# Attention in two-part float32: scores computed once with queries on the partitions, probabilities transposed on TensorE

## The chip, the cores and the metric

The kernel runs on one core of a Trainium2 chip. The metric is the device time of one execution in microseconds, as the median of several runs. The trace shown here is one profiled execution. PE is TensorE (the matrix engine), DVE is VectorE, ACT is ScalarE, POOL is GpSimd, SP is the engine that issues DMAs.

## The reference

The input is x of shape (2, 1024, 256). It is normalised over its last axis (xn). Two branches read xn, and both are added to x:

```python
# attention: 16 heads of 192 (128 without rotation, 64 with rotary embedding)
q_latent, kv_latent = xn @ wq_down, xn @ wkv_down        # 192 and 64 wide
q = concat([q_latent @ wq_nope, rope(q_latent @ wq_rope)])
k = concat([kv_latent @ wk_nope, rope(kv_latent @ wk_rope)])
v = kv_latent @ wv_up
scores = q k^T / sqrt(192), masked causally
out = softmax(scores) @ v                                # per head
attention = out.reshape(b, t, 16 * 192) @ wo
# feed-forward: 32 experts of 96, top 8 by a softmax over gate logits
ffn = sum over experts of routing * (silu(xn @ gate) * (xn @ up)) @ down
```

## The kernel before

The work has three blocks, one after the other: `prepare` (line 69: normalisation, transposes, the latents), `attend` (line 399: attention, and the routing weights beside it) and `mix` (line 1103: the experts). Only `attend` and small parts of `prepare` are touched.

**Numbers in two parts.** Where float32 precision is wanted from a fast product, a tensor is kept as a high part (type float32r, written by a copy on ACT) and a low part (what is left, a subtraction on DVE or POOL). A product is then three matmuls: high with high, high with low, low with high. A matmul whose operands are plain float32 takes two records in the trace and twice the time for a column.

**Folded weights.** For a head, the key's part without rotation is folded into the query's projection, so that scores without rotation are a product of a 64-wide folded query with the 64-wide key-value latent. With the 64 rotated rows this makes 128 rows, one full contraction. Values are the latent itself (`kvn`, 64 wide); the value weights are folded with `wo`.

**Stages.** A stage is one pair of heads (eight pairs) and one batch element (two): sixteen stages `s`. Pair 0 and the last pair are written out, pairs 1 to 6 are a loop. In a stage PE goes through 12 steps (`step_of`, line 347), each for one block of 128 keys and a chunk of up to 512 queries, keys on the partitions: for either head a score product of three matmuls (lines 599 to 601), a bfloat16 product that subtracts the row maximum from the whole column (line 598: ones times a diagonal matrix of maxima), and on the diagonal a mask product (line 597). ACT takes the exponential into a ring of three buffers (line 734). The values product (line 613) of the step before follows, both heads at once in two 64-column halves of the array. DVE and POOL add the probabilities of the two heads into `first` (lines 908 and 1060); a product with ones gives the row sums (line 634), DVE takes the reciprocal of 128x512 (line 913) and multiplies (line 917).

**Maxima.** They are wanted before the step's scores. So each stage also computes, for the next one, a high-with-high score product with queries on the partitions, in 24 pieces of up to 512 keys (line 566, mask in line 569), whose maximum DVE takes (line 897); ACT turns them into the diagonal matrices (line 770). `PIECE_AT` (line 378) says by hand after which step each piece stands. The first stage's 24 pieces run before the loop.

**Side work.** Between the steps stand products for the next stage, by the table `SIDE` (line 382): QR0, QR1 (rotated query of chunk 0 and 1), KR0, KR1 (rotated key), QL0, QL1 (folded query), L0 and Lp (row sums of chunk 0, and of chunk 1 of the stage before), Y0, Y1, Yp0, Yp1 (output products), B and WA (weight folds, in every other stage). They alternate between two PSUM banks `ps_x`; each waits until the one two before it is consumed. A rotated product is consumed by DVE (lines 850 and 851), then POOL (lines 1029 and 1031), then split by ACT (lines 757 and 758) and POOL (line 1047). A folded query is split by ACT (lines 750 and 751) and DVE (lines 858 and 860). WA is consumed by DVE in lines 867 to 872, B in lines 877 and 879, output products in line 923.

Every engine works through its own queue in the order in which its function of the block is written.

Of the kernel before, what the change touches and what calls it, by code (L numbers as in the profile page):

```python
# [26 lines left out]
AXX = mybir.AxisListType.X  # L27
# [7 lines left out]
P = 128  # L35
# [33 lines left out]
def prepare(nc, d, keep):  # L69

    ctx = ExitStack()
    with ctx:
# [22 lines left out]
        def _(sp):  # L95
# [7 lines left out]
            for name, to in (("cos", keep["cosv"]), ("sin", keep["sinv"]), ("ones", keep["ones"]), ("mask", keep["raw_mask"])):  # L103
                sp.dma_start(to[:, :], d[name]).then_inc(ahead_loaded, 16)
# [6 lines left out]
            sp.wait_ge(ahead_loaded, 16 * 6)  # L111

        @block.vector
        def _(dve):
# [27 lines left out]
            def low_parts(g):  # L142
# [4 lines left out]
                for count, lo, ps, hi in (  # L147
# [6 lines left out]
                    nc.vector.tensor_tensor(lo, ps, hi.bitcast(F32), ALU.subtract).then_inc(lo_done, 1)  # L154

            def split_first_weights():

                dve.wait_ge(ahead_loaded, 16 * 6)
# [22 lines left out]
        def _(act):  # L181
# [14 lines left out]
            for g in range(NCH):  # L196
# [8 lines left out]
                nc.scalar.activation(keep["kv"][:, s], ps_l[2][:, :], ACT.Copy).then_inc(hi_copied, 1)  # L205
                nc.scalar.activation(keep["khi"][b][0][64:P, cs], ps_l[2][64:P, :], ACT.Copy).then_inc(hi_copied, 1)
                nc.scalar.activation(keep["khi"][b][1][0:64, cs], ps_l[2][0:64, :], ACT.Copy).then_inc(hi_copied, 1)
# [4 lines left out]
                if g == 1:  # L212

                    act.wait_ge(ident_loaded, 16)
                    act.wait_ge(ahead_loaded, 16 * 6)
                    for to, of in (("ident16", "ident"), ("ones16", "ones"), ("mask16", "raw_mask")):
                        nc.scalar.activation(keep[to][:, :], keep[of][:, :], ACT.Copy).then_inc(consts16_done, 1)
# [6 lines left out]
        def _(pe):  # L224
# [13 lines left out]
            for g in range(NCH):  # L238
# [18 lines left out]
                if g == 1:  # L257
# [3 lines left out]
                    pe.wait_ge(ahead_loaded, 16 * 6)  # L261
# [26 lines left out]
STEPS = 12  # L288
PROLOGUE = ["QR0", "KR0", "QL0", "QR1", "KR1", "QL1"]
STAGE = ["QR0", "KR0", "QR1", "KR1", "Lp", "QL0", "QL1", "L0", "Yp0", "Yp1", "B", "WA", "Y0", "Y1"]  # L290


def misc_order(first=False, last=False):
# [3 lines left out]
    for b in range(B):  # L297
        for name in STAGE:
# [4 lines left out]
            got.append((b, name))  # L303
    return got
# [7 lines left out]
def misc(i, b, name):  # L312

    if b is None:
        n = PROLOGUE.index(name)
        return n, n % 2
    if isinstance(i, int) and i == 0:
        n = len(PROLOGUE) + FIRST.index((b, name))
        return n, n % 2
    if isinstance(i, int) and i == PAIRS - 1:  # L320
        n = BEFORE_LAST + LAST.index((b, name))
        return n, n % 2
    pos = LATER.index((b, name))
    if isinstance(i, int):
        n = AFTER_FIRST + len(LATER) * (i - 1) + pos
        return n, n % 2
    return i * len(LATER) + (AFTER_FIRST - len(LATER) + pos), (AFTER_FIRST + pos) % 2


def misc_predecessor(i, b, name):  # L330

    if b is None:
        at = PROLOGUE.index(name) - 2
        return (0, None, PROLOGUE[at]) if at >= 0 else None
    if isinstance(i, int) and i == 0:
        at = FIRST.index((b, name)) - 2
# [1094 lines left out]
```

## Time and profile before

| | us |
|---|---|
| median of 3 runs (1276.21 to 1277.69) | 1276.71 |
| the profiled execution, its own time | 1277.71 |
| its span, first to last instruction | 1275.9 |
| mean granted clock of TensorE | 0.985 |

The span is what the rows show; 1.8 us lie around it. A matmul's recorded duration includes its way through the array and overlaps the next one: what it costs is read from the distance between starts. Names in the rows leave buffer numbers out, and the tile `keys` is a first buffer that holds `khi` and `klo` of batch 0, `xtf` holds the shuffled half of a rope product, and `t` is `t1`.

### The profile page before, as it was taken

The numbers are of one execution on the slowest core, as the hardware profiler recorded it, in microseconds if no ns is written. First come the engines' busy times: TensorE is split into PE (matmuls) and PEld (weight loads), VectorE is DVE, ScalarE is ACT, GpSimd is POOL, SyncE is SP. The second block draws the span as 40 slices with busy tenths as digits, with TensorE's granted clock in tenths as the row PEclk, the third lists the DMA queues.
The fourth block names the chain that finished last, engine by engine and source line by source line (L and its number), as shares of the span: only waits on it lengthen the run. The fifth ranks groups of instructions, "written<-read, shape, count | busy, mean of one in ns | idle before, by whom it ended". The sixth has DMA issues, their size and how long they took to land. (4 is left out here: it accounts for less than half of the span.)

```text
span 1275.9 us, 20266 instructions
## 1 busy us (share of the span) xinstructions
PE 1216.7 (95%) x5952; PEld 809.1 (63%) x5952; DVE 898.6 (70%) x1410; ACT 589.5 (46%) x1192; POOL 682.0 (53%) x546
## 2 busy tenths in 40 slices
PE   5899899999999999999999999979999999999997
PEld 3555465555565555555655555547888887888886
DVE  6679879879889888888888798664544444544444
ACT  3454536545546445456355365443434343333332
POOL 1176667677677667767776676552233333233332
PEclk9988999999999999999999999998999999999999
DMA  5001001001000000000000001006533334433332
GB/s 202 34 1 33 1 1 33 1 1 32 0 0 17 15 0 15 16 0 2 30 0 0 15 0 58 1 26 180 163 115 107 110 115 114 127 109 115 115 115 90
DMA packets 26442, 67.33 MB, mean 53 GB/s; under 512 B 3044, under 2 KB 9700, under 8 KB 26408
## 3 DMA queue, kind: packets, MB, share of 16 engines
q1 hardware_dynamic: 26264, 66.84, 17.4%
q8 instruction: 17, 0.28, 0.1%
q14 instruction: 17, 0.14, 0.0%
q10 hardware_dynamic: 144, 0.07, 0.0%
HBM read 62.42 MB, written 4.47 MB: 52 GB/s over the span
## 5 line engine op out<-in xcount | busy, mean ns | idle before, releaser
L734 ACT ACTIVATE ring<-ps_s 128x512 f32<-128x512 f32 (+3 forms) x320 | 146.5, 468 | 302.3 <-PE ps_s L601 301.2
L1333 POOL TENSOR_TENSOR hl<-hf,hh 128x512 fp32r<-128x512 f32 x96 | 123.5, 1286 | 288.2 <-ACT hh L1270 288.2
L897 DVE TENSOR_REDUCE nm<-ps_m 128x1 f32<-128x512 f32 (+3 forms) x370 | 197.8, 550 | 47.0 <-PE ps_m L569 42.1
L1060 POOL TENSOR_TENSOR first<-first,ring 128x512 f32<-128x512 f32 (+3 forms) x160 | 159.5, 997 | 83.8 <-ACT ring L734 51.2
L1029 POOL TENSOR_TENSOR xtf<-xtf,sinv 128x512 f32<-128x512 f32 x62 | 85.3, 1375 | 119.3 <-DVE xtf L851 119.3
L1302 DVE TENSOR_TENSOR gs<-gs,routing 128x512 f32<-128x512 f32 x64 | 44.3, 692 | 137.8 <-ACT gs L1266 137.8
L908 DVE TENSOR_TENSOR first<-first,ring 128x512 f32<-128x512 f32 (+3 forms) x160 | 133.1, 832 | 9.7 <-ACT ring L734 4.9
L613 PE MATMUL ps_o<-ring,kvn 128*64 128x512 f32 (+3 forms) x640 | 132.6, 493 | 0.0
L598 PE MATMUL ps_s<-shift,ones 128*128 128x512 bf16 (+3 forms) x384 | 126.7, 330 | 0.2 <-ACT first L734 0.2
L1270 ACT ACTIVATE hh<-hf 128x512 fp32r<-128x512 f32 x96 | 60.7, 633 | 122.0 <-DVE hf L1307 122.0
L1266 ACT ACTIVATE gs<-ps_g 128x512 f32<-128x512 f32 x96 | 57.4, 598 | 121.4 <-PE ps_g L1225 121.4
L913 DVE RECIPROCAL rec<-ps_x 128x512 f32<-128x512 f32 x32 | 107.3, 3354 | 5.1 <-PE ps_x L634 3.1
L1047 POOL TENSOR_TENSOR qlo<-t,qhi 64x512 fp32r<-64x512 f32 x64 | 94.9, 1483 | 8.6 <-POOL first L1060 2.6
L599 PE MATMUL ps_s<-qhi,keys 128*128 128x512 f32 (+1 forms) x192 | 93.2, 485 | 0.0
L599 PE MATMUL ps_s<-qhi,khi 128*128 128x512 f32 (+1 forms) x192 | 92.1, 480 | 0.0
L1031 POOL TENSOR_TENSOR t<-t,xtf 128x512 f32<-128x512 f32 x62 | 84.5, 1362 | 4.9
L850 DVE TENSOR_TENSOR t<-ps_x,cosv 128x512 f32<-128x512 f32 x64 | 44.2, 691 | 57.1 <-PE ps_x L550 57.1
L566 PE MATMUL ps_m<-khi,qhi 128*128 128x512 f32 (+1 forms) x192 | 73.5, 393 | 7.6 <-DVE nm L897 7.6
L1064 POOL TENSOR_TENSOR olo<-on,ohi 128x512 fp32r<-128x512 f32 x31 | 42.4, 1368 | 70.0 <-ACT ohi L782 70.0
L1307 DVE TENSOR_TENSOR hf<-gs,ps_u 128x512 f32<-128x512 f32 x96 | 66.1, 688 | 10.6 <-PE ps_u L1225 1.3
L566 PE MATMUL ps_m<-keys,qhi 128*128 128x512 f32 (+3 forms) x178 | 68.3, 397 | 5.2 <-DVE nm L897 4.8
L566 PEld LDWEIGHTS ps_m<-khi,qhi 128*128 128x128 f32 x192 | 36.6, 191 | 55.4 <-DVE nm L897 45.7
(241 smaller groups left out, 3104.3 us busy)
## 6 DMA issues: line engine op xcount, KB each, us to landing
routing<-wT_scratch SPq DMA_DIRECT2D x34, 256.0 KB, 3.7
raw_a<-in_e SPq DMA_DIRECT2D x17, 384.0 KB, 3.0
cosv<-in_e SPq DMA_DIRECT2D x17, 384.0 KB, 3.0
sinv<-wT_scratch SPq DMA_DIRECT2D x17, 384.0 KB, 3.6
raw<-in_e SPq DMA_DIRECT2D x17, 384.0 KB, 3.0
routing<-wT_scratch SPq DMA_DIRECT2D x16, 384.0 KB, 3.3
raw_a<-in_a SPq DMA_DIRECT2D x8, 512.0 KB, 3.4
raw_b<-in_b SPq DMA_DIRECT2D x8, 480.0 KB, 4.0
```

The lines of the kernel that those rows point to most:

```text
L566: mm = nc.tensor.matmul(out[:, 0:keys], qhi[b][e][:, t * P:(t + 1) * P], khi[b][e][:, k0:k0 + keys], start=True, stop=not diagonal)
L598: nc.tensor.matmul(out[:, off:], ones16[:, :], shift[:, c, e, off:], start=not diagonal, stop=False, skip_group_check=True)
L599: nc.tensor.matmul(out[:, off:], khi[b][e][:, kk], qhi[b][e][:, q], start=False, stop=False, skip_group_check=True)
L613: nc.tensor.matmul(ps_o[64 * e:64 * e + 64, off:], kvn[:, b * 8 + j, :], probs(k, e), start=j == 0, stop=last).then_inc(pv_done, 1)
L734: nc.scalar.activation(probs(k, e), ps_s[(2 * k + e) % 3][:, off:], ACT.Exp, scale=SCALE).then_inc(exp_done, 1)
L897: nc.vector.tensor_reduce(out=to, in_=bank[:, 0:keys], axis=AXX, op=ALU.max, negate=True).then_inc(piece_max, 1)
L908: nc.vector.tensor_tensor(first[:, c, 0, off:], first[:, c, 0, off:], probs(k, 0), ALU.add).then_inc(sum_dve, 1)
L913: nc.vector.reciprocal(rec[:, :], ps_x[x][:, :]).then_inc(rec_done, 1)
L1029: nc.gpsimd.tensor_tensor(sh[:, g, :], sh[:, g, :], sinv[:, c * CH:(c + 1) * CH], ALU.mult).then_inc(rope_sin, 1)
L1047: nc.gpsimd.tensor_tensor(lo[to_b][e][rows, cs], t1[rows, g, :], hi[to_b][e][rows, cs].bitcast(F32), ALU.subtract).then_inc(rope_lo, 1)
L1060: nc.gpsimd.tensor_tensor(first[:, c, 1, off:], first[:, c, 1, off:], probs(k, 1), ALU.add).then_inc(sum_pool, 1)
L1333: nc.gpsimd.tensor_tensor(hl[:, c, :], hf[:, c, :], hh[:, c, :].bitcast(F32), ALU.subtract).then_inc(h_lo, 1)
```

## The change

Scores are computed once, with queries on the partitions. A stage now goes through eight tiles `t` of 128 queries; for each head all keys up to the diagonal stand side by side in two PSUM banks (two halves from tile 4 on), three matmuls to a half. DVE takes one negated maximum over the row, ACT the exponential with it as bias and with its sum accumulated in the same instruction. In the next tile PE transposes the probabilities in blocks of 128, ACT copies those of one bank (`ps_t[0]`) and DVE those of the other (`ps_t[1]`) into `pt`, and one values product for each key block and head follows. The reciprocals of the sums (128 by 16 numbers) are widened on ACT, transposed on PE (L0 and Lp now) and copied on ACT. The pieces, the shift products, the sums on DVE and POOL, `first`, `ring` and `shift` are gone. Side work has one bank `ps_x`, each waiting for the one just before it; the six of the prologue have banks of their own. The scale of the scores is put on the key-value latent in `prepare`; the constant `ones` is no longer loaded. The transposes of the routing weights take the places of the last stage's first four projections. `mix` is unchanged.

The diff, cut to its core:

```diff
-                nc.scalar.activation(keep["kv"][:, s], ps_l[2][:, :], ACT.Copy).then_inc(hi_copied, 1)
+                nc.scalar.activation(keep["kv"][:, s], ps_l[2][:, :], ACT.Copy, scale=SCALE).then_inc(hi_copied, 1)
...
+            def scores(i, b, t, e, half):
+                s = i * 2 + b
+                u = s * U + 2 * t + e
+                halves = halves_of(t)
+                if half == 0:
+                    ge(pe, exp_done, u - 1)
...
+                if diagonal:
+                    nc.tensor.matmul(out[:, width - P:width], mask16[:, :], ident16[:, :], start=True, stop=False, skip_group_check=True)
+                nc.tensor.matmul(out[:, 0:width], qhi[b][e][:, q], khi[b][e][:, kk], start=not diagonal, stop=False, skip_group_check=True)
+                nc.tensor.matmul(out[:, 0:width], qhi[b][e][:, q], klo[b][e][:, kk], start=False, stop=False, skip_group_check=True)
+                mm = nc.tensor.matmul(out[:, 0:width], qlo[b][e][:, q], khi[b][e][:, kk], start=False, stop=True, skip_group_check=True)
+            def turn(s, t, e, g):
+                x = g if t >= TPC else e
+                before = s * TURNS_PER_S + turns_before(t) + (e if t >= TPC else 0)
+                pe.wait_ge(exp_done, s * U + 2 * t + e + 1)
+                ge(pe, copied[x], before)
+                for at, j in enumerate(groups_of(t)[g]):
+                    mm = nc.tensor.transpose(ps_t[x][:, at * P:(at + 1) * P], prob[t % 2][e][:, j * P:(j + 1) * P], ident[:, :])
+                mm.then_inc(turned[x], 1)
+            def values(s, b, t):
+                for x in range(2):
+                    pe.wait_ge(copied[x], s * TURNS_PER_S + turns_before(t + 1))
+                if t % TPC == 0:
+                    ge(pe, on_done, s * 2 + t // TPC)
+                at = slice(t % TPC * P, (t % TPC + 1) * P)
+                for j in range(t + 1):
+                    for e in range(2):
+                        mm = nc.tensor.matmul(ps_o[64 * e:64 * e + 64, at], kvn[:, b * 8 + j, :], pt[t % 2][:, e, j, :], start=j == 0, stop=j == t)
...
+                    for t in range(TILES):
+                        sp, bp, tp = before_tile(i, b, t)
+                        has = earlier or t > 0
+                        if t == 0:
+                            scores(i, b, t, 0, 0)
+                            if has:
+                                turn(sp, tp, 0, 0)
+                                turn(sp, tp, 0, 1)
+                            scores(i, b, t, 1, 0)
+                            also("Lp")
+                            if has:
+                                turn(sp, tp, 1, 0)
+                                turn(sp, tp, 1, 1)
+                                values(sp, bp, tp)
+                            also("QR0")
+                        elif t < TPC:
+                            scores(i, b, t, 0, 0)
+                            turn(sp, tp, 0, 0)
+                            turn(sp, tp, 1, 0)
+                            scores(i, b, t, 1, 0)
+                            values(sp, bp, tp)
+                            also(("KR0", "QL0", "QR1")[t - 1])
+                        elif t == TPC:
+                            scores(i, b, t, 0, 0)
+                            turn(sp, tp, 0, 0)
+                            scores(i, b, t, 0, 1)
+                            also("L0")
+                            turn(sp, tp, 1, 0)
+                            scores(i, b, t, 1, 0)
+                            scores(i, b, t, 1, 1)
+                            values(sp, bp, tp)
+                            also("Yp0")
+                        else:
+                            scores(i, b, t, 0, 0)
+                            turn(sp, tp, 0, 0)
+                            scores(i, b, t, 0, 1)
+                            turn(sp, tp, 0, 1)
+                            also(("KR1", "Yp1", "WA")[t - TPC - 1])
+                            scores(i, b, t, 1, 0)
+                            turn(sp, tp, 1, 0)
+                            turn(sp, tp, 1, 1)
+                            scores(i, b, t, 1, 1)
+                            if t == TILES - 1:
+                                also("Y0")
+                            values(sp, bp, tp)
+                            also(("QL1", "B", "Y1")[t - TPC - 1])
...
+                nc.scalar.activation(prob[t % 2][e][:, 0:len(halves) * width].rearrange("p (h k) -> p h k", k=width),
+                                     ps_s[e][:, 0:len(halves), 0:width], ACT.Exp, bias=nm[:, e:e + 1],
+                                     accum_out=lsum[:, t // TPC, t % TPC, e:e + 1]).then_inc(exp_done, 1)
...
+                nc.vector.tensor_reduce(out=nm[:, e:e + 1], in_=ps_s[e][:, 0:len(halves), 0:halves[0][1]], axis=AXXY, op=ALU.max,
+                                        negate=True).then_inc(max_done, 1)
...
+                nc.vector.tensor_copy(pt[t % 2][:, e, blocks[0]:blocks[-1] + 1, :].rearrange("p j q -> p (j q)"),
+                                      ps_t[1][:, 0:len(blocks) * P]).then_inc(copied[1], 1)
...
+                nc.vector.tensor_tensor(on[:, :], ps_o[:, :], rec[:, :], ALU.mult).then_inc(on_done, 1)
```

TPC is 4, TILES is 8, and in names like QR0 the digit is the chunk. `sp, bp, tp` is the tile before. From tile 5 on, and in tile 0, the blocks of the tile before are turned in two groups for each head, the first into `ps_t[0]` and the second into `ps_t[1]`; for the tiles 0 to 3 there is one group for each head, head 0's into `ps_t[0]` and head 1's into `ps_t[1]`. `values` waits for all of them.

The order that the new functions give the other engines in a tile:

- ACT: `widen` (tiles 0 and 4); the copy from `ps_t[0]` of head 0; the exponential of head 0; `take_reciprocals` (0 and 4); the copy from `ps_t[0]` of head 1 (0 and 5 to 7); the exponential of head 1; then `out_hi` (1 and 6), `latent_hi` (2 and 5), `rope_hi`, which is four split copies (4 and 7).
- DVE: `invert` (0 and 4); `latent_low(1)` (6); the maximum of head 0; one copy from `ps_t[1]`; the rope products of KR1 (5), the addition of Yp1 (6), the split of WA (7, batch 0); the second copy from `ps_t[1]` (5 to 7); the maximum of head 1; the second copy (0); `normalise` (0 and 4); the rope products of QR0, KR0, QR1 (0, 1, 3) or `latent_low(0)` (2); the additions of Yp0 (4), Y0 and Y1 (7), the split of B (6, batch 0).
- POOL: `rope_sum` 0, `out_low` of the stage before, `rope_sum` 1 and 2, `rope_low` 0 and 1, `rope_sum` 3, `out_low`, `rope_low` 2 and 3.

## Rows read from the trace of the kernel before

**Rows 1.** The page, part 1: busy us, share of the span, instructions.

```profile
PE 1216.7 (95%) x5952; PEld 809.1 (63%) x5952; DVE 898.6 (70%) x1410; ACT 589.5 (46%) x1192; POOL 682.0 (53%) x546
```

**Rows 2.** Line 885 alone: its count, durations, first and last start.

```profile
L885 DVE TENSOR_TENSOR nm1c<-nm x16: 160/160/195, 74.8 to 818.6; 128x8 f32<-128x8 f32 x16
```

**Rows 3.** Stretches: length, each engine busy (instructions), granted clock, DMA share, GB/s.

```profile
49.40:75.00 25.60, 18.52 (x64) 11.91 (x64) 21.62 (x45) 11.12 (x21) 15.32 (x12) 0.80 0.07 21
...
129.60:818.60 689.00, 671.93 (x3522) 392.76 (x3521) 585.78 (x870) 355.52 (x784) 487.38 (x392) 1.00 0.04 11
...
818.60:852.80 34.20, 34.20 (x190) 18.92 (x189) 18.91 (x19) 20.12 (x42) 16.68 (x13) 1.00 0.09 24
```

**Rows 4.** Timeline, around 573 us: start us, us, engine line operation out<-in.

```profile
573.04 0.38 PE L598 MATMUL ps_s<-shift,ones 128*128 128x512 bf16 x1
...
573.73 0.39 PE L601 MATMUL ps_s<-qhi,keys 128*128 128x512 f32 x1
...
573.96 0.40 PE L550 MATMUL ps_x<-q1hi,rhi 128*128 128x512 f32 x1
...
574.15 0.60 ACT L734 ACTIVATE first<-ps_s 128x512 f32<-128x512 f32 x1 [2.43 <-PE ps_s L601]
```

**Rows 5.** Timeline of PE around 570 us.

```profile
570.22 0.28 PE L600 MATMUL ps_s<-qlo,khi 128*128 128x128 f32 x1
...
570.33 0.28 PE L601 MATMUL ps_s<-qhi,klo 128*128 128x128 f32 x1
...
570.45 0.45 PE L566 MATMUL ps_m<-keys,qhi 128*128 128x512 f32 x1
...
570.80 0.22 PE L597 MATMUL ps_s<-mask,ident 128*128 128x128 bf16 x1
```

**Rows 6.** Timeline of PE around two value groups, of 128 and of 512 columns.

```profile
626.48 0.44 PE L613 MATMUL ps_o<-ring,kvn 128*64 128x128 f32 x4
...
626.85 0.50 PE L550 MATMUL ps_x<-kv,rhi 128*128 128x512 f32 x1
...
630.18 1.08 PE L613 MATMUL ps_o<-first,kvn 128*64 128x512 f32 x4
...
631.19 0.50 PE L550 MATMUL ps_x<-kv,rhi 128*128 128x512 f32 x1
```

**Rows 7.** Timeline of PE, eight transposes; line 1202 alone, durations in ns.

```profile
23.57 1.04 PE L234 MATMUL ps_t<-ident,xn 128*128 128x128 f32 x8
...
L1202 PE MATMUL ps_tr<-ident,yacc x32: 270/273/328, 1090.9 to 1271.2; 128*128 128x128 f32 x32
```

**Rows 8.** Groups of DVE by form: busy us, mean ns, idle before.

```profile
L897 DVE TENSOR_REDUCE nm<-ps_m 128x1 f32<-128x512 f32 x184 | 124.3, 686 | 24.2 <-PE ps_m L569 19.9 <-PE ps_m L566 2.8
...
L897 DVE TENSOR_REDUCE nm<-ps_m 128x1 f32<-128x128 f32 x62 | 17.6, 284 | 8.7 <-PE ps_m L569 8.6
...
L851 DVE STREAM_SHUFFLE xtf<-ps_x 128x512 f32<-128x512 f32 x64 | 47.2, 738 | 0.0
...
L850 DVE TENSOR_TENSOR t<-ps_x,cosv 128x512 f32<-128x512 f32 x64 | 44.2, 691 | 57.1 <-PE ps_x L550 57.1
...
L867 DVE CAST rhi<-raw_a 128x384 fp32r<-128x384 f32 x7 | 8.9, 1268 | 0.0
...
L877 DVE CAST bhi<-ps_x 128x256 fp32r<-128x256 f32 x8 | 3.4, 422 | 1.6 <-PE ps_x L530 1.6
```

**Rows 9.** Groups of ACT by form: busy us, mean ns, idle before.

```profile
L734 ACT ACTIVATE ring<-ps_s 128x512 f32<-128x512 f32 x128 | 72.9, 594 | 112.0 <-PE ps_s L601 111.5
...
L757 ACT ACTIVATE qhi<-t 64x512 fp32r<-64x512 f32 x32 | 20.1, 627 | 0.7 <-DVE t L936 0.3
...
L823 ACT ACTIVATE q1hi<-xtf 128x1024 fp32r<-128x1024 f32 x1 | 1.1, 1051 | 0.0
```

**Rows 10.** Two stretches on which the granted clock fell; columns as in rows 3.

```profile
109.70:114.30 4.60, 1.68 (x6) 0.38 (x5) 4.60 (x7) 1.76 (x5) 3.56 (x3) 0.92 0.35 116
...
114.30:120.30 6.00, 5.96 (x20) 3.96 (x20) 5.41 (x38) 1.88 (x6) 1.70 (x2) 0.50 0.00 0
```

More of the change, by code:

```diff
@@ L284 @@
 ROUTED = 16 * 2
-STEPS = 12
+TILES = T // P
 PROLOGUE = ["QR0", "KR0", "QL0", "QR1", "KR1", "QL1"]
-STAGE = ["QR0", "KR0", "QR1", "KR1", "Lp", "QL0", "QL1", "L0", "Yp0", "Yp1", "B", "WA", "Y0", "Y1"]
+STAGE = ["Lp", "QR0", "KR0", "QL0", "QR1", "L0", "Yp0", "KR1", "QL1", "Yp1", "B", "WA", "Y0", "Y1"]
+TURNS = ["W0", "W1", "W2", "W3"]
 def misc_order(first=False, last=False):
@@ L303, in misc_order @@
             got.append((b, name))
+            if last and b and name == "Lp":
+                got += [(b, turn) for turn in TURNS]
     return got
@@ L627, in row_sums, with spread @@
-            def row_sums(i, b, name, s, c):
-                for e in range(2):
-                    pe.wait_ge(*sums(s, c, 7 if c else 3, e))
-                def products(out):
-                    for e in range(2):
-                        mm = nc.tensor.matmul(out[64 * e:64 * e + 64, :], ones[:, 0:64], first[:, c, e, :], start=True, stop=True)
+                        mm = nc.tensor.transpose(out[0:E, j * P:(j + 1) * P], w2[:, g * TPC + j, :], ident[:, :])
                     return mm
                 side(i, b, name, products)
+            def spread(out):
+                for t in range(TPC):
+                    mm = nc.tensor.transpose(out[:, t * P:(t + 1) * P], rec[:, t * P:(t + 1) * P], ident[:, :])
+                return mm
@@ L694, in _ @@
             for name in PROLOGUE:
                 project(0, None, name, 0, 0)
-            for n in range(NP):
-                piece(0, n, 0)
             pairs_loop(pe, body)
-            s = 2 * PAIRS - 1
-            values(s, 1, STEPS - 1, alone=True)
-            n = BEFORE_LAST + len(LAST)
+            s, t = 2 * PAIRS - 1, TILES - 1
             for e in range(2):
-                pe.wait_ge(*sums(s, 1, 7, e))
+                for g in range(2):
+                    turn(s, t, e, g)
+            pe.wait_ge(widened, s * 2 + 2)
@@ L822, in body @@
                             act.wait_ge(keep["xT_loaded"], 16)
[L823 to L824 removed]
+                            nc.scalar.activation(keep["xhi"][t - 4][:, 0:ROUND], keep["xtf"][:, t - 4, :], ACT.Copy).then_inc(keep["x_hi"], 1)
+                        if not more and t == TILES - 1:
                             act.wait_ge(keep["w_loaded"][0], 16)
```

694 lines of the change are left out of this document (300 added, 394 removed).

## The prediction

> **What bounds the kernel now.** I read the page first: PE is busy for 95% of the span, DVE for 70% [rows 1]. A busy share does not say what a stage costs, so I cut the span. One small DVE operation (line 885) runs once in each of the sixteen attention stages (one head pair and one batch element each), from 74.8 to 818.6 us [rows 2]; between the second and the last lie 14 stages in 689 us, 49.2 each, with DVE busy for 41.8, ACT for 25.4, POOL for 34.8 of them [rows 3]. The start of attention takes 25.6 us and the last stage 34.2 [rows 3]. The change touches nothing in the block of the experts behind attention. Then I took PE's cost from starts, not from durations. A 512-column product in two-part float32 holds its slot 0.23 us (lines 601 and 550), a whole 512 step with the shift product 0.92, so the shift 0.23 [rows 4]. 128 columns cost 0.11 (384 and 256 lie between, 0.17 and 0.12); a 512 piece for the maxima with its mask 0.35 [rows 5]. A value step of both heads costs 1.01 for 512 columns but 0.37 for 128, where by proportion 0.21 is due: each group has a fixed part of some 0.2 for entering and leaving the two 64-column halves [rows 6]. A transpose costs 0.11, eight starts in 1.04 with one duration of 0.27 at the end, so (1.04 - 0.27) / 7 [rows 7]. Adding all work of a stage so (scores 13.0, shifts 4.0, pieces with masks 6.6, score masks 1.1, values 10.7, row sums 2.2, projections 5.5, output products 2.8, weight folds 1.0) gives 46.9. PE waits only 2.3 us a stage: it is the bound.
>
> **PE work, part by part (per stage).** Removed: shifts 4.0, pieces 6.6, the row sums 2.2. Scores keep their columns (4608 a head, three products) and 24 groups: 14.6 with masks against 14.1. Values: the same columns, but 36 key blocks of 128 for each pair; inside one group I take 0.22 for a block (the proportion), and 8 groups instead of 12: 36 x 0.22 + 8 x 0.2 = 9.5. Ends: 0.21 and the 0.37 of a lone block [rows 6]; the first is nearer, since what the lone block pays is entry and exit. Added: 72 transposes of probabilities x 0.11 = 7.9 and 8 of reciprocals = 0.9. The rest stays. Sum: 14.6 + 9.5 + 7.9 + 10.2 (reciprocals 0.9, projections 5.5, outputs 2.8, folds 1.0) = 42.2, 4.7 less than before. If the waits stayed at 2.3, a stage would take 44.5.
>
> **Other engines.** DVE loses the adds, the 3.4 us reciprocals and the pieces, and gains 16 maxima over whole rows and 14 copies. From 512 columns in 0.69 and 128 in 0.28 [rows 8] a maximum of 1024 takes 1.22. A copy out of PSUM of 256 columns takes 0.42 (line 877) [rows 8], so 512 take 0.69. ACT: an exponential 0.59 for 512, a 1024-column pass 1.05, a split copy 0.63 [rows 9]; with the accumulated sum I add 0.1 (ends 0 and 0.3). By this DVE is busy some 33 us a stage and ACT 29: neither is a bound by its sum. POOL loses its adds (about 10 us) and has slack; the order of its rope sums and splits puts each ahead of its reader by my count. The scale on the latent copies, one DMA of constants fewer, and the removed first load cost nothing: they lie in the prologue beside other work.
>
> **The waits are the point.** Before, values of step k-1 needed only an exponential of long ago. Now a tile's values need four or fewer copies, half of them on DVE, and DVE works in order: side work stands ahead of them. I walk one stage; a hand-over costs 0.2 each way (the exponential starts 0.2 behind the slot of line 601 [rows 4]; the other way I take the same, ends 0.1 and 0.3). A rope step on DVE takes 0.69 + 0.74 = 1.43 [rows 8].
> Tile 1: at the end of QR0 DVE starts the rope (0.2 to 1.65), then the maximum (2.07), then the copy (2.35); values may start at 2.5. PE has only 1.16 us of scores and transposes: wait 1.35.
> Tile 2: the same behind KR0: 0.2 + 1.43 + 0.55 + 0.42 + 0.16 = 2.8 against 1.7: 1.1.
> Tile 3: behind QL0 ACT first splits (1.2), then DVE subtracts (1.4), then maximum 0.69 and copy 0.55: 4.04 against 2.26: 1.8.
> Tile 4: behind QR1 rope, inversion 0.25, widening on ACT 0.6: the transposed reciprocals wait 1.3, with 0.1 at the values: 1.4.
> Tile 5: the copy on ACT stands behind four rope splits (2.5): 0.5, and KR1's rope ahead of the second copy: 0.7. Tile 6: QL1's subtraction holds the single side bank for 1.0 and the copies 0.2. Tile 7: in every other stage the weight split (1.27 for its first cast [rows 8], with three smaller operations some 2.7) stands ahead of the last copy: 1.5, else 0.7.
> Tile 0: ACT has the rope splits (2.5) ahead of the widening and two copies: 1.2 before the reciprocals, 0.2 before the transposes, 1.06 before the values: 2.4.
> Together 11.5 a stage, 42.2 + 11.5 = 53.7, or 4.5 more than 49.2. In this walk PE waits for DVE, though DVE is busy for under two thirds of it.
>
> **A rule against a row.** The copy is the dearest link. Line 877's 256 columns in 0.42 are what a 1x rate from PSUM gives (the slope of 1.05 ns a column of line 897 and its fixed part) [rows 8]; I take that. The Trainium skill, VectorE: DVE Perf Modes, the perf-mode tier table, allows a copy with PSUM up to the 2x mode; by that, as an estimate, copies would shrink by up to 0.27 each, some 1.5 us of the waits of a stage and 24 us in all, 1313 instead of 1337. The row decides.
>
> **Sum.** Middle: 14 x 4.5 = +63. The first stage has no earlier tile to finish: -5. Prologue: the 24 pieces go, but PE then waits for POOL's first two splits, so only 5.5 of the 25.6 us come off. Last stage: 34.2 now, as it has no pieces and no projections; new work 37.5 plus 6 of waits: +9. The tail gives back 1. Total +61 on the profiled execution's 1277.7; that stands 1.0 over the median of 1276.7, so 1337 for the median. Ends: hand-overs 0.1 less or more over some eight waits (13 us each way), accumulate and copy (20).
>
> **Rivals.** (a) The waits hide. If DVE and ACT got to the copies in time, PE would be the bound at 44.5 a stage: 14 x -4.7, -8, -5.5, +2: 1277.7 - 77, about 1200. It decides from the point where waits fall under 7.0 a stage (49.2 - 42.2). For it: DVE and ACT have free time. Against: in seven of eight tiles side work is written ahead of the copy. Half-way cases give 1240 to 1270.
> (b) The clock falls. From 109.7 to 114.3 us PE had 1.68 us of work in 4.60, and the granted clock then stood at 0.50 (1.2 of 2.4 GHz) for 6 us [rows 10]. At the start of tile 0, between the second score group and the values, PE has in 3.7 us only twelve transposes, 1.3 us. If the clock falls there, the values (2.0) and QR0 (1.15) run at half speed: 1.7 to 3.2 more a stage, 1364 to 1388. Against it: stretches with fewer gaps show 1.00 in all 14 stages [rows 3]. The Trainium skill, TensorE: Matmul & The Clock Gate, Part 4: PE-mode transpose, says that transposes do not count as activity in the way products do. By that the stretch would look idle; no row here has transposes alone for that long.
> (c) The lone-block price holds for each block: 0.37 instead of 0.22, 36 x 0.15 = 5.4 a stage, 1423.
> (d) It comes out even, gain and waits cancelling within 0.2%, about what a measurement of this kernel can tell from no change.
>
> **Chances.** Forecast 0.50 (1305 to 1360), clock 0.20, hidden waits 0.20, lone-block price 0.07, even 0.03. Likeliest 1337. The range of 1250 to 1390 leaves out the lower two thirds of (a) and (c). Faster 0.20, same 0.03, slower 0.77.
>
> **What would show it.** Right: stage length near 54; PE's work by starts near 42; DVE named as the releaser of PE's weight loads of the values, largest in tiles 0 and 3, with the rope and latent subtractions before the copy; DVE copy of 512 near 0.69; transposes 0.11 apart; attention starts near 69.5 us. Wrong: a stage under 49 with few waits for the copies (then my in-order walk is at fault), blocks of values 0.37 apart, or a granted clock under 1.00 in each stage.

## The result, and the profile after

| | before | after |
|---|---|---|
| median, us | 1276.5 | 1313.9 (1312.1 to 1316.1, 4 runs) |
| ratio, 95% interval | | 1.0292 (1.0274 to 1.0310) |
| span of the profiled execution, us | 1275.9 | 1312.6 |

The change makes the kernel 37 us slower; 1337 was forecast, inside a range of 1250 to 1390. First the page of the changed kernel, part 1 (the answer to [rows 1]).

```profile
PE 1161.8 (89%) x7616; PEld 936.2 (71%) x7616; DVE 720.3 (55%) x1298; ACT 646.2 (49%) x1287; POOL 493.9 (38%) x386
```

PE, DVE and POOL all do less than before, and the span is longer: the time has gone into idle PE. A stage now begins with the first mask of line 545; the stretches cut there are the start of attention's first stage, the 14 middle stages, the last 13 of those (a steady rhythm), the last stage, the tail, and the experts. Columns as in [rows 3].

```profile
69.30:117.30 48.00, 41.41 (x307) 33.03 (x308) 30.35 (x68) 24.67 (x55) 21.75 (x17) 0.96 0.07 22
117.30:849.00 731.70, 632.53 (x4978) 509.69 (x4978) 431.45 (x803) 405.67 (x870) 322.54 (x252) 0.99 0.03 10
173.10:849.00 675.90, 585.89 (x4630) 471.83 (x4630) 395.74 (x714) 375.93 (x807) 298.39 (x234) 0.99 0.04 11
849.00:890.80 41.80, 39.30 (x342) 32.70 (x342) 22.09 (x36) 27.87 (x60) 12.42 (x8) 1.00 0.07 20
890.80:901.70 10.90, 6.70 (x59) 4.97 (x58) 5.80 (x9) 3.17 (x7) 0.00 (x0) 0.89 0.00 1
901.70:1312.60 410.90, 400.10 (x1760) 328.59 (x1760) 189.32 (x266) 156.13 (x243) 123.45 (x96) 0.99 0.41 122
```

A steady stage takes 675.9 / 13 = 52.0 us, with DVE busy for 30.4, ACT for 28.9 and POOL for 23.0 of them, and PE idle for (675.9 - 585.9) / 13 = 6.9. The same 13 stages of the kernel before, cut at the same place in the work:

```profile
180.30:817.60 637.30, 623.53 (x3278) 364.93 (x3277) 542.68 (x806) 330.14 (x728) 452.44 (x364) 1.00 0.04 12
```

That is 49.0 a stage and 1.1 of idle PE. The whole difference of the spans, 36.7, is made of: the prologue -5.7 (attention starts at 69.3, not 75.0), the first stage -5.6, the middle 14 stages +42.7, the last stage +6.6, the tail -2.1, the experts +0.8.

What PE waits for, from the view of waits (us in total, times, the longest), PE first, then its weight loads:

```profile
PE ps_o L571 <- DVE pt L875: 49.5, 47, 1.7
PE ps_x L589 <- ACT rec L731: 23.5, 28, 2.4
...
PE ps_x L598 <- DVE qlo L844: 11.7, 14, 1.7
```

```profile
PEld ps_o L571 <- ACT pt L724: 51.2, 71, 1.1
```

Line 571 is the values product, `pt` the copied transposes, line 589 the transposed reciprocals, line 598 an output product that needs the side bank. The longest wait, 1.7, comes once a stage, in tile 3:

```profile
448.36 0.40 PE L520 MATMUL ps_x<-q1hi,llo 128*128 128x512 f32 x1
...
448.79 0.59 ACT L743 ACTIVATE qhi<-ps_x 64x512 fp32r<-64x512 f32 x1 [1.03 <-PE ps_x L520]
...
449.41 0.59 ACT L744 ACTIVATE qhi<-ps_x 64x512 fp32r<-64x512 f32 x1
...
450.03 0.68 DVE L842 TENSOR_TENSOR qlo<-ps_x,qhi 64x512 fp32r<-64x512 f32 x1 [2.98 <-ACT qhi L744]
...
450.63 0.40 PE L548 MATMUL ps_s<-khi,qlo 128*128 128x512 f32 x1
450.75 0.69 DVE L844 TENSOR_TENSOR qlo<-ps_x,qhi 64x512 fp32r<-64x512 f32 x1
451.47 0.69 DVE L866 TENSOR_REDUCE nm<-ps_s 128x1 f32<-128x512 f32 x1
452.08 0.55 DVE L875 COPY pt<-ps_t 128x384 f32<-128x384 f32 x1
...
452.77 0.88 PE L571 MATMUL ps_o<-pt,kvn 128*64 128x128 f32 x12 [1.74 <-DVE pt L875]
```

Read it upwards. The values start at 452.77 behind the copy, the copy behind a maximum, the maximum behind two subtractions of side work, those behind two splits on ACT, and these behind QL0, which PE issued one tile ago. The transposes that the copy reads had long been written: nothing about them was late. This is the in-order queue of the forecast.

Not each wait is of this kind. In tile 0 PE waits 1.0 for the copies too (438.02 us), but DVE had stood idle for 1.72 us before the last one (437.19 to 437.88): nothing of side work was ahead of it. There the wait is the hand-over and the copy itself, with no independent product on PE to put between the transposes and the values. So the cause has two parts, side work ahead of copies, and copies that nothing on PE covers.

### The profile page after: what moved, and what is told of

Its sections match the earlier page's. It is cut to its first block and busy times, and to the rows that moved or that the text cites. A ratio compares the mean times of both kernels' runs of the same rounds, so it can differ in the third digit from the quotient of the medians.

```text
span 1312.6 us, 23292 instructions
## 1 busy us (share of the span) xinstructions
PE 1161.8 (89%) x7616; PEld 936.2 (71%) x7616; DVE 720.3 (55%) x1298; ACT 646.2 (49%) x1287; POOL 493.9 (38%) x386
## 5 line engine op out<-in xcount | busy, mean ns | idle before, releaser
L714 ACT ACTIVATE prob<-ps_s,nm 128x128 f32<-128x128 f32 (+7 forms) x256 | 189.5, 740 | 203.3 <-DVE nm L866 200.9
L866 DVE TENSOR_REDUCE nm<-ps_s 128x1 f32<-128x128 f32 (+7 forms) x256 | 192.3, 751 | 70.5 <-PE ps_s L548 69.0
L571 PE MATMUL ps_o<-pt,kvn 128*64 128x128 f32 x2304 | 154.0, 277 | 64.5 <-DVE pt L875 49.5
L571 PEld LDWEIGHTS ps_o<-pt,kvn 128*64 128x64 f32 x2304 | 126.2, 136 | 100.9 <-ACT pt L724 51.2
L559 PE MATMUL ps_t<-ident,prob 128*128 128x128 f32 x1152 | 173.0, 276 | 9.4 <-DVE pt L875 6.7
L559 PEld LDWEIGHTS ps_t<-ident,prob 128*128 128x128 f32 x1152 | 138.7, 142 | 32.2 <-issue 10.9
L724 ACT ACTIVATE pt<-ps_t 128x128 f32<-128x128 f32 (+2 forms) x192 | 96.6, 503 | 88.1 <-PE ps_t L559 86.7
L875 DVE COPY pt<-ps_t 128x128 f32<-128x128 f32 (+2 forms) x192 | 101.6, 529 | 56.2 <-PE ps_t L559 55.3
L546 PE MATMUL ps_s<-khi,qhi 128*128 128x384 f32 (+4 forms) x192 | 78.5, 409 | 0.0
L546 PE MATMUL ps_s<-keys,qhi 128*128 128x384 f32 (+4 forms) x192 | 78.2, 407 | 0.0
```

Source lines behind the costliest of these rows:

```text
L546: nc.tensor.matmul(out[:, 0:width], qhi[b][e][:, q], khi[b][e][:, kk], start=not diagonal, stop=False, skip_group_check=True)
L559: mm = nc.tensor.transpose(ps_t[x][:, at * P:(at + 1) * P], prob[t % 2][e][:, j * P:(j + 1) * P], ident[:, :])
L571: mm = nc.tensor.matmul(ps_o[64 * e:64 * e + 64, at], kvn[:, b * 8 + j, :], pt[t % 2][:, e, j, :], start=j == 0, stop=j == t)
L714: nc.scalar.activation(prob[t % 2][e][:, 0:len(halves) * width].rearrange("p (h k) -> p h k", k=width), ps_s[e][:, 0:len(halves), 0:width] ...
L724: nc.scalar.activation(pt[t % 2][:, e, blocks[0]:blocks[-1] + 1, :].rearrange("p j q -> p (j q)"), ps_t[0][:, 0:len(blocks) * P], ACT.Copy ...
L866: nc.vector.tensor_reduce(out=nm[:, e:e + 1], in_=ps_s[e][:, 0:len(halves), 0:halves[0][1]], axis=AXXY, op=ALU.max, negate=True).then_inc( ...
```

## The experiments

All are edits of the changed kernel. Each was timed beside runs of the kernel before; its ratio is to that kernel, as is the changed kernel's own 1.0292. The theory: PE waits for copies that stand behind side work in the in-order queues of DVE and ACT, or that nothing on PE covers. The rivals: PE's own added work makes the time; or the one side bank does, and a wait only moves.

**e1_swap.** PE issues the side product ahead of the values.

```diff
-                            values(sp, bp, tp)
                             also(("KR0", "QL0", "QR1")[t - 1])
+                            values(sp, bp, tp)
...
-                        if t == 0 and earlier:
-                            normalise(s - 1, 1)
                         if more and t in (0, 1, 3):
                             rope_products(i, b, ("QR0", "KR0", None, "QR1")[t], s + 1)
+                        if t == 0 and earlier:
+                            normalise(s - 1, 1)
```

(Tile 0 is changed in the same way, with QR0 ahead of its values.)

> In tiles 0 to 3 TensorE issues the side product (QR0, KR0, QL0, QR1: 1.27, 0.57, 1.27, 1.26 us in the trace of the changed kernel) ahead of the values product instead of behind it, and VectorE takes the rope step of QR0 ahead of the normalisation. Theory (TensorE waits for copies that stand behind side work on VectorE and ScalarE, and for nothing else there): the waits ahead of the values products, 1.0, 1.0, 0.7 and 1.9 us in tiles 0 to 3, find cover. Up to 4.5 us a stage go, 15 stages, so 1314 - 67 = 1247 (1235 to 1265). Rival (TensorE's own added work, transposes and values, makes the time): the same instructions are issued, so 1314 stays, within 5. Second rival (the one side bank): a side product then finds the bank held by the rope step of the one before and the wait only moves in front of it: 1300 to 1318.

Measured 1231.1 us, ratio 0.9639 (0.9623 to 0.9655): the same instructions in another order are 83 us faster than the changed kernel, more than the theory's range allowed (1235 to 1265), and faster than the kernel before. Tile 3 again, now of e1:

```profile
412.81 0.40 PE L548 MATMUL ps_s<-khi,qlo 128*128 128x512 f32 x1
412.96 0.69 DVE L867 TENSOR_REDUCE nm<-ps_s 128x1 f32<-128x512 f32 x1
...
413.04 0.44 PE L520 MATMUL ps_x<-q1hi,rhi 128*128 128x512 f32 x1
...
413.57 0.55 DVE L876 COPY pt<-ps_t 128x384 f32<-128x384 f32 x1
...
414.34 0.63 PEld L571 LDWEIGHTS ps_o<-pt,kvn 128*64 128x64 f32 x12 [0.36 <-issue]
414.34 0.88 PE L571 MATMUL ps_o<-pt,kvn 128*64 128x128 f32 x12
```

QR1 fills the time in which DVE takes the maximum and the copy, and the values wait for nothing. The steady 13 stages (columns as in [rows 3]):

```profile
164.10:770.30 606.20, 576.25 (x4629) 466.62 (x4628) 398.17 (x714) 376.24 (x807) 299.89 (x234) 1.00 0.04 13
```

46.6 a stage, 5.4 less where 4.5 was expected. The distances between starts explain most of the surplus: QR1's rope step also comes earlier, and the reciprocals of tile 4 with it (0.5). Some 0.2 or 0.3 more is clock: the changed kernel has two stretches of half clock in these 13 stages (shown further on), e1 stands at 1.00. The busy times of PE, DVE and ACT change by 2% at most. The rival of PE's own work is out; so is that of the side bank, for this order.

**e2_dve_order.** DVE's order alone.

```diff
                             maximum(s, t, 0)
                             take_turned(sp, tp, 1, 0)
+                            if more and t in (1, 2):
+                                rope_products(i, b, ("QR0", "KR0")[t - 1], s + 1)
+                            if more and t == 3:
+                                latent_low(i, b, 0, s + 1, 1 - b)
```

> VectorE's order alone: the rope steps of QR0 and KR0 and the latent subtraction of QL0 move behind the maximum and the copy of the tile that follows. TensorE's order stays. Theory (single side bank beside the in-order queue): the copies come in time, but the next side product waits until the rope step has read the bank. By hand: KR0 is due 10.0 us into the stage and the rope step of QR0 would end at 10.8, QR1 is due at 18.7 and the subtraction ends at 19.1. So of 3.6 us of waits in tiles 1 to 3 only some 1.5 go: 1314 - 15 x 1.5 = 1292 (1283 to 1305). Rival (VectorE's order is the whole cause): 15 x 3.6 = 54 off, 1260. Rival (TensorE's work): 1314.

Measured 1292.3, ratio 1.0114 (1.0097 to 1.0131), the theory's number. Tile 1: the values go at once, and the wait stands in front of KR0, whose bank the rope step still reads.

```profile
435.49 0.44 PE L571 MATMUL ps_o<-pt,kvn 128*64 128x128 f32 x4
436.69 0.50 PE L520 MATMUL ps_x<-kv,rhi 128*128 128x512 f32 x1 [0.76 <-DVE xtf L835]
```

So the side bank is the second half of the cause: side work cannot simply be put off. What helps is cover on PE.

**e9_norm_first.** The same point inside e1: only DVE's two lines of e1 are put back (normalisation ahead of the rope step).

> e1 with one thing put back: in tile 0 VectorE normalises (behind the values) ahead of the rope step of QR0, as in the changed kernel. TensorE's order is e1's. Theory (side work must be off the one side bank before the next side product): the values end 7.3 us into a stage, the normalisation and the rope step then run to 9.5, KR0 is due at 8.5, so it waits 1.1 to 1.3: 15 of them, 17 to 20 over e1's 1231, 1249 (1245 to 1254). Rival (only TensorE's order matters): 1231 within 3.

Measured 1249.0, ratio 0.9782 (0.9766 to 0.9798), the theory's number: 18 us over e1, and still 65 under the changed kernel. KR0 waits again:

```profile
412.53 0.50 PE L520 MATMUL ps_x<-kv,rhi 128*128 128x512 f32 x1 [0.81 <-DVE xtf L836]
```

**e3_rope_hi.** ACT's four splits of chunk 1 move into the next stage, behind tile 0.

```diff
-                        if more and t == TILES - 1:
-                            rope_hi(s + 1, 1, 1 - b)
+                        if t == 0 and earlier:
+                            rope_hi(s, 1, b)
```

> ScalarE's four split copies of the second chunk (2.6 us) move from the end of a stage, where they stand ahead of the widening and of the copies of tile 0, to behind the exponentials of tile 0 of the next stage. Theory: in tile 0 the widening starts 0.8 us earlier, the transposed reciprocals and all behind them too: 0.8 x 15 = 12 off, 1302 (1297 to 1307); the wait of 1.0 ahead of the values of tile 0 stays, since the last copy on VectorE follows the same transposes as before. Rival (ScalarE's splits are hidden there, the inversion on VectorE ends last): 1314 within 3.

Measured 1306.2, ratio 1.0233 (1.0216 to 1.0250): 8 us off where 12 were expected. The wait of the reciprocals for the widening falls from the 23.5 above to

```profile
PE ps_x L589 <- ACT rec L731: 14.2, 19, 2.4
```

and its steady stage is 0.8 shorter (665.7 / 13 = 51.2), as priced. The shortfall is in the main one wait in the last stage, at 849.81 us, which the edit makes itself. POOL's splits follow ACT's moved ones and end late; ACT's copy of the routing weights waits 4.4 for the last of them, and the copy that PE's values need stands behind it. The longest wait of that kind is 0.2 in the changed kernel; in e3 it is 3.7:

```profile
PE ps_o L571 <- ACT pt L724: 6.2, 13, 3.7
```

**e4_no_sums.** The exponentials accumulate nothing.

```diff
-                                     ps_s[e][:, 0:len(halves), 0:width], ACT.Exp, bias=nm[:, e:e + 1],
-                                     accum_out=lsum[:, t // TPC, t % TPC, e:e + 1]).then_inc(exp_done, 1)
+                                     ps_s[e][:, 0:len(halves), 0:width], ACT.Exp, bias=nm[:, e:e + 1]).then_inc(exp_done, 1)
```

> Leaves out the row sums: the exponentials accumulate nothing, and the reciprocals are taken from eight columns of the router logits instead, so that the output is not normalised. What goes is the accumulation's price on ScalarE: 0.09 us of each exponential and a read of the accumulator of 0.19 behind it, 256 times, 72 us of ScalarE's time. Theory (ScalarE is not the bound, and only a few of its exponentials have a copy of theirs behind them that TensorE waits for): 0.3 us a stage, 1309 (1300 to 1314). Rival (ScalarE is on the path in most tiles): most of the 72 us go, 1245 to 1270.

Measured 1311.6, ratio 1.0273 (1.0256 to 1.0290), 2 us less than the changed kernel, whose interval overlaps with this one. Whether anything was gained is not shown; that the rival's 44 to 69 us were not is, so ACT is not the bound. Of its price, one part of the expectation fell. Groups of ACT by form, the changed kernel, then e4:

```profile
L714 ACT ACTIVATION_READ_ACCUMULATOR prob<-ps_s,nm 128x1 f32 x256 | 49.8, 194 | 0.0
...
L714 ACT ACTIVATE prob<-ps_s,nm 128x512 f32<-128x512 f32 x32 | 22.0, 687 | 30.2 <-DVE nm L866 30.2
```

```profile
L714 ACT ACTIVATE prob<-ps_s,nm 128x512 f32<-128x512 f32 x32 | 22.0, 688 | 31.6 <-DVE nm L865 31.6
```

The accumulation costs the read behind it, 0.19, and nothing in the exponential. The 0.09 by which a 512-column exponential is longer than in [rows 9] (594 ns) is there without it. The other thing that is new in it is the bias, read from a tensor; that this is its price was not tried.

**e5_all, e6_ql1, e10_all_mended.** What e1 leaves. e6 adds the first of these edits to e1, e5 all of them:

```diff
+                            if t == TPC + 1:
+                                also("QL1")
                             values(sp, bp, tp)
-                            also(("QL1", "B", "Y1")[t - TPC - 1])
+                            if t > TPC + 1:
+                                also(("QL1", "B", "Y1")[t - TPC - 1])
...
-                            also("L0")
                             turn(sp, tp, 1, 0)
                             scores(i, b, t, 1, 0)
+                            also("L0")
...
+                            if t == TILES - 1:
+                                take_turned(sp, tp, 0, 1)
                             maximum(s, t, 0)
-                            if has:
+                            if has and t < TILES - 1:
                                 take_turned(sp, tp, 0, 1)
```

(and e3's edit).

> e1 and one move more: QL1 ahead of the values in tile 5. Theory: the values of tile 5 find their copies in time (0.4), and QL1 reaches the split and the subtraction 1.24 us earlier, so Yp1 in tile 6 no longer waits for the side bank (0.9): 1.3 x 15 = 20 off, 1211 (1207 to 1217). Rival (QL1 waits for the rope step of KR1, so that only its place changes): 1228 to 1233.

Measured 1219.5, ratio 0.9542 (0.9527 to 0.9557): 12 off, not 20. The wait for the side bank at Yp1, 11.7 in 14 waits above, is down to one:

```profile
PE ps_x L598 <- DVE qlo L848: 1.9, 1, 1.9
```

but a stage is only 1.0 shorter (44.9 and 46.3 by turns where e1 has 45.9 and 47.3), 13 in all for the 14 middle stages (656.3 us in e1, 643.2 here). The block of the experts, which the edit does not touch, took 409.5 us in this trace and 407.7 in e1's, so a part of what is lost outside the middle is not the edit's.

> All moves together, on the changed kernel: e1's order (side product ahead of the values in tiles 0 to 3), e3's (ScalarE's splits of the second chunk behind tile 0 of the next stage), the transposed reciprocals of tile 4 behind one more score group, QL1 ahead of the values in tile 5, and in tile 7 VectorE's copy ahead of its maximum. Theory: what is left of waits in e1's trace, a stage: 1.0 ahead of the reciprocals of tile 0, 0.3 in tile 4, 0.4 ahead of the values and 0.3 ahead of a score group in tile 5, 0.9 ahead of Yp1 in tile 6, 0.6 at the transposes of tile 7 in every other stage. Some 3.0 a stage go: 1231 - 45 = 1186 (1180 to 1200), a stage of 43.7, which is TensorE's own work. Rival (the waits move on to other places, since ScalarE and VectorE form a chain of their own through maximum, exponential and copy): 1215 to 1232.

Measured 1212.8, ratio 0.9496 (0.9478 to 0.9514), between theory and rival. Two reasons stand in its trace: one wait that e3's edit makes in the last stage, where a copy on ACT waits 4.4 for POOL's last split, which comes late behind ACT's moved ones, and PE waits for the copy (4.1 us at line 582, the transposed routing weights),

```profile
PE ps_x L582 <- ACT t L767: 4.1, 1, 4.1
```

and a copy put ahead of the maximum in tile 7, which took the wait from the transposes and put 0.4 or 0.8 of it further on, by turns. e10 mends both. It leaves out the move in tile 7, and its other edits are:

```diff
-                        if t == 0 and earlier:
+                        if t == 0 and earlier and more:
                             rope_hi(s, 1, b)
...
-                            also(("KR1", "Yp1", "WA")[t - TPC - 1])
+                            also(("KR1", "Yp1", "Y0" if b else "WA")[t - TPC - 1])
...
+                        if t == TPC + 2:
+                            out_hi(s, 0, misc(i, b, "Yp1") if earlier else None)
                         exponent(s, t, 1)
```

(Y0 and the output split are taken out of their old places in the tile; for the last stage the rope split keeps its place at the end of the stage before.)

> e5_all with what its trace shows as left. The last stage keeps ScalarE's splits of the second chunk at the end of the stage before (in e5_all the last stage waited for them, 4.1 us once at line 582); tile 7 has its maximum ahead of the copy again, and in every other stage Y0 stands between the transposes of tile 7, with ScalarE's output split ahead of the second exponential of tile 6 so that Y0 is ready. Theory: -4.8 for the last stage, and the waits of tile 7 (0.4 in one kind of stage, 0.8 in the other) go, 15 x 0.6 = 9: 1213 - 13 = 1200 (1195 to 1207). Rival (the wait of tile 7 comes from the length of the chain maximum, exponential, transposes, and turns up elsewhere): 1207 to 1214.

Measured 1199.9, ratio 0.9404 (0.9388 to 0.9419): 6% under the kernel before, and the fastest of all. Its steady stages:

```profile
160.60:737.80 577.20, 571.46 (x4629) 466.32 (x4628) 397.50 (x714) 374.99 (x808) 299.30 (x234) 1.00 0.04 13
```

44.4 a stage, with 0.4 of idle PE. The theory's 1200 was met, but not term by term: a steady stage is 0.4 shorter than in e5_all (44.8), where 0.6 was expected for tile 7. It is also the time of rival (a) of the prediction, 44.5 a stage and about 1200, reached by order alone; its two parts were others (42.2 of work and 2.3 of waits there, 43.7 and 0.7 here).

**e7_turns_twice.** With the waits gone, what do the transposes cost?

```diff
-                for at, j in enumerate(groups_of(t)[g]):
+                for at, j in list(enumerate(groups_of(t)[g])) * 2:
```

> e5_all with every transpose of probabilities issued twice into the same bank (the result is the same): 72 more a stage. Theory (with the waits gone TensorE is the bound, and transposes cost 0.109 each wherever they stand): 16 x 72 x 0.109 = 126 over e5_all, less what the last waits take in; 105 to 130 over it. Rival (transposes hide behind the chain of maximum, exponential and copy): under 40 over it.

Measured 1335.8, ratio 1.0465 (1.0449 to 1.0481): 123 over e5_all, in the theory's range and three times the rival's. So PE is the bound there. But 123 / 1152 = 0.107 for each added transpose is in part luck. e7 has five idle stretches of PE at the start of a stage, once in each turn of the loop, 2.5 to 3.2 us each and 13.9 in all, which e5_all has not. The profile names nobody that PE waited for, and their cause is open:

```profile
490.68 0.23 PE L545 MATMUL ps_s<-ident,mask 128*128 128x128 bf16 x1 [2.58 <-issue]
```

Half clock behind some of them adds more. With both taken off, steady stages are 6.2 longer than e5_all's, 0.086 for each of the 72; if e5_all's waits of about 1 us a stage are filled, it is 0.10. From start to start a transpose inside a group takes 0.109 in both (median).

**e8_pool_beside.** More work on GpSimd beside DVE's weight split.

```diff
                     out_low(s, 0)
+                    if b == 0 and not is_last(i):
+                        for n in range(3):
+                            ge(pool, dum_done, i * 3 + n)
+                            nc.gpsimd.tensor_tensor(dum[0][:, :], sinv[:, 0:CH], sinv[:, CH:2 * CH], ALU.mult).then_inc(dum_done, 1)
```

> The changed kernel with three more multiplications of 512 columns on GpSimd behind its output split, in every other stage, 21 in all, which nobody reads; they run while VectorE casts the weights (line 850). Theory for the cast, forecast at 1.27 us and measured at 0.35: an SBUF-only cast on VectorE waits for the GpSimd operation that is under way. Then rows of the cast go from 0.35 up to between 0.6 and 1.5, ending some 0.2 behind the end of a GpSimd operation. Rival (the cast's 1.27 before had another cause): it stays 0.35. For the time: at most 7 x 1.2 = 8 us more than 1314 by the theory, 0 by the rival.

The cast alone, of the changed kernel and of e8 (least, median, most, in ns), and a stretch of e8's timeline:

```profile
L850 DVE CAST rhi<-raw_a x7: 350/351/352, 112.2 to 740.5; 128x384 fp32r<-128x384 f32 x7
```

```profile
L851 DVE CAST rhi<-raw_a x7: 715/718/1166, 113.8 to 746.5; 128x384 fp32r<-128x384 f32 x7
```

```profile
534.95 4.01 POOL L1065 TENSOR_TENSOR dum<-sinv 128x512 f32<-128x512 f32 x3
...
537.08 0.72 DVE L851 CAST rhi<-raw_a 128x384 fp32r<-128x384 f32 x1
```

Six of the seven casts start 0.5 before a GpSimd operation ends, and end 0.2 after it; the seventh starts 0.95 before and ends 0.22 after. The cast waits for that operation, then takes its time. The subtraction behind it, which reads two tensors of SBUF, goes from 0.56 to 1.20. Time: 1319.4, ratio 1.0333 (1.0313 to 1.0352), 5 more than the changed kernel.

## Why the prediction was right, and where its sizes were off

**Direction and mechanism: right.** A steady stage is PE's work plus its waits. By the distances between starts the work is 43.7 and the waits 8.3; forecast were 42.2 and 11.5. (The 6.9 of idle PE is less than the waits, since a matmul's recorded duration reaches into the wait behind it.) Tile by tile:

| tile | waits forecast | measured |
|---|---|---|
| 0 | 2.4 | 1.9 |
| 1 | 1.35 | 1.0 |
| 2 | 1.1 | 0.7 |
| 3 | 1.8 | 1.9 |
| 4 | 1.4 | 0.8 |
| 5 | 1.2 | 0.6 |
| 6 | 1.2 | 1.1 |
| 7 | 1.5 or 0.7 | 0 or 0.6 |

**The terms that were mis-sized.** The middle gave 42.7 instead of 63, and that is nearly the whole miss of 23 us.

(1) Chains on DVE were summed by durations. "A rope step on DVE takes 0.69 + 0.74 = 1.43" is the step that was mis-sized: tile 1 shows what a link costs.

```profile
441.38 0.69 DVE L834 TENSOR_TENSOR t<-ps_x,cosv 128x512 f32<-128x512 f32 x1 [0.66 <-PE ps_x L520]
...
442.00 0.72 DVE L835 STREAM_SHUFFLE xtf<-ps_x 128x512 f32<-128x512 f32 x1
442.63 0.41 DVE L866 TENSOR_REDUCE nm<-ps_s 128x1 f32<-128x256 f32 x1
442.95 0.28 DVE L875 COPY pt<-ps_t 128x128 f32<-128x128 f32 x1
```

From start to start 0.62, 0.63 and 0.32, against durations of 0.69, 0.72 and 0.41: 0.07 to 0.09 less a link. Three links make 0.25 of the 0.35 by which tile 1 was too dear. PE's cost had been taken from starts; DVE's had not. It is no rule for all links: in tile 3 above, the operations behind the two subtractions start 0.03 after the recorded end (450.03, 450.75, 451.47). That tile's forecast of 1.8 came out near the 1.9 measured; its sum of 4.04 had no hand-over at its end, and 4.18 was measured from the end of QL0 to the values.

(2) The weight split of tile 7: "1.27 for its first cast". It took 0.35, since GpSimd no longer works beside it, and no wait was left in that stage. e8 shows the reason, and so does the trace of before:

```profile
508.79 1.28 POOL L1064 TENSOR_TENSOR olo<-on,ohi 128x512 fp32r<-128x512 f32 x1
...
509.01 1.27 DVE L867 CAST rhi<-raw_a 128x384 fp32r<-128x384 f32 x1
```

All seven casts there start beside a GpSimd operation and end 0.2 behind its end. The row of [rows 8] was of a cast that waited, and the forecast carried the wait along with it.

(3) PE's work was 1.5 too low. The slots inside a group were right (0.23 for 512 columns, transposes 0.11, a block of values 0.22, with 0.15 a group where 0.2 was taken), but the first product of a group costs about 0.1 more, 0.32 for 512 columns:

```profile
476.91 0.47 PE L546 MATMUL ps_s<-khi,qhi 128*128 128x512 f32 x1
477.22 0.39 PE L547 MATMUL ps_s<-klo,qhi 128*128 128x512 f32 x1
477.45 0.39 PE L548 MATMUL ps_s<-khi,qlo 128*128 128x512 f32 x1
```

So scores came to 15.4 (14.6 forecast), projections to 6.3 (5.5), output products to 3.2 (2.8), less 0.5 for the values. The change did not bring this: a stage has 24 groups of scores before and after, and by the same distances the kernel before spends 6.0 on projections and 3.1 on output products. The forecast took 0.23 for every product, though behind the values of [rows 6], where a group starts at 626.85, the next product starts 0.34 later:

```profile
627.19 0.40 PE L550 MATMUL ps_x<-kv,rlo 128*128 128x512 f32 x1
```

For the scores it is new: in the kernel before, a bfloat16 product opened each group, and with the one behind it took 0.45 (573.04 to 573.49), two plain slots.

The waits were 3.2 a stage too dear, and (3) gave 1.5 back; that the two partly cancel is luck. Of the 3.2, (2) is 0.75 (1.5 in every other stage), and (1) some 0.25 each in tiles 1 and 2 and 0.2 in tiles 4 and 5. The rest, about half of it, in tiles 0, 4 and 5 above all, was not taken apart; a part of tile 4 is that the widening on ACT starts 0.03 behind the inversion on DVE (456.48 to 456.51).

**Point by point.** Attention starts at 69.3 (69.5 forecast). First stage -5.6 (-5). Last stage +6.6 (+9), tail -2.1 (-1). DVE is busy for 30.4 a stage (33), ACT for 28.9 (29). The hand-over from PE was the 0.20 taken (454.84 to 455.04); the one back to PE was 0.13 to 0.15, and between DVE and ACT 0.03. The accumulated sum, for which the forecast took 0.1 from no row, costs the read of 0.19. DVE was named as forecast for the values' matmuls (49.5 in all) and the waits are largest in tiles 0 and 3; for their weight loads, of which the forecast spoke, the view names ACT and no DVE (51.2). DVE's maximum and copy, by form:

```profile
L866 DVE TENSOR_REDUCE nm<-ps_s 128x1 f32<-128x1024 f32 x32 | 39.1, 1222 | 31.8 <-PE ps_s L548 31.8
...
L875 DVE COPY pt<-ps_t 128x512 f32<-128x512 f32 x48 | 33.2, 692 | 47.7 <-PE ps_t L559 47.3
```

Both are as forecast. The estimate of 1313 by the tier table is next to the result, but not for its reason: the copy runs at the 1x rate. The Trainium skill, VectorE: DVE Perf Modes, under "Why PSUM operands drop a tier", says that float32 with an operand in PSUM stays at 1x, which narrows the table's entry; the row agrees with that section.

**The rivals.** (a) had the right length of a stage, though for another order. Its condition, waits under 7.0 a stage, missed by 1.3 (with the work as it was, 43.7, it was 5.3, and missed by 3.0); that cheap moves of order could bring them near nothing was not seen, though the forecast named side work ahead of the copy as the obstacle. (b) happened now and then, not in each stage. The steady stages stand at a mean clock of 0.99, with two drops:

```profile
558.00:561.40 3.40, 3.40 (x14) 3.00 (x13) 1.43 (x4) 0.68 (x2) 0.72 (x1) 0.50 0.00 0
553.50:558.00 4.50, 2.76 (x23) 2.04 (x22) 3.13 (x5) 2.25 (x6) 0.00 (x0) 1.00 0.00 0
```

PE had been busy for 2.76 of 4.50 us, and then ran at half clock (1.2 of 2.4 GHz) for 3.4. (c) is out: a block costs 0.22 inside a group.

## What to carry to other kernels

When a change turns a wait for something old into a wait for something fresh, walk each queue in order and ask what PE can do in the meantime; here the same instructions took 1314 or 1200 us, and e1 gave 83 of the 114: 65 by putting the independent product ahead of the dependent one (e9), 18 by the order on DVE that frees the side bank in time. Moving work on the engine that is late helps only as far as the buffers that it holds allow. Price chains by starts, PE's and the other engines', and take no duration from a row without asking what ran beside it.

## What the runs showed of the hardware

An SBUF-to-SBUF float32 cast on DVE of 384 columns takes 0.35 us alone and ends 0.2 us behind the GpSimd operation under way when it is issued beside one (0.72 to 1.17 in e8, 1.27 in [rows 8]); a cast out of PSUM shows nothing of it (256 columns, 0.41 right behind the cast in e8, 0.42 in the changed kernel). The Trainium skill, GPSIMD Engine Reference, 1. Specifications, says that GpSimd shares its SBUF interfaces with VectorE, and that VectorE contends in its two-port modes or with two inputs in SBUF; the subtraction of e8, with two inputs in SBUF, agrees. The cast has one input; that it runs in a two-port mode fits its 0.35, where the same columns take 0.55 out of PSUM, but was not shown.

With the transposes issued twice the granted clock fell more often (mean 0.977 to 0.982 in the four runs of e7, 0.985 to 0.991 in the five of e5_all). e7, two stretches on end:

```profile
491.80:495.20 3.40, 3.40 (x19) 3.34 (x17) 0.93 (x2) 0.95 (x3) 0.00 (x0) 0.50 0.00 0
488.00:491.80 3.80, 1.22 (x12) 1.13 (x12) 1.14 (x3) 0.63 (x1) 0.00 (x0) 1.00 0.02 4
```

Here too a stretch with little work on PE came first (1.22 of 3.80, with the idle 2.58 shown above), so no run shows that transposes alone bring the clock down.
